# Cross attention and mixture of experts on one core: scores in three PSUM banks, steps of up to 1536 columns, two score buffers for three

## The reference

```
q = ln(x) @ Wq;  k, v = split(concat(ctx, ln(x)) @ Wkv)      # 1178 keys, 1024 queries
dots = einsum('bhid,bhjd->bhij', q, k) * 16**-0.5
dots = where(j > i + 154, -inf, dots)                        # key j is seen from query j-154 on
x = x + softmax(dots) @ v @ Wout + bout
probs = softmax(ln(x) @ Wg);  each expert takes its 256 best tokens, each token goes to one expert
x = x + weight * (gelu(ln(x) @ W1[e]) @ W2[e])
```

## Time and profile before

| | us |
|---|---|
| median of 3 runs (lowest, highest) | 389.99 (389.31, 390.83) |
| profiled execution: its time | 389.28 |
| profiled execution: span from first to last instruction | 387.4 |
| PE busy | 351.4 (91%) |
| ACT busy | 266.4 (69%) |
| DVE busy | 209.8 (54%) |
| POOL busy | 114.8 (30%) |
| ACTIVATE of `exps` (L845), 192 instructions | 169.0 |
| matmuls of `scores` (L1086) / of `values` (L1107) | 101.4 / 96.9 |

### The profile page before, as it was taken

One profiled execution on the slowest core, in us unless ns is written; L12 is line 12 of the kernel. 1 busy time (PEld: TensorE's weight loads), 2 busy tenths in 40 slices (PEclk: granted clock), 3 DMA queues, 4 the chain that ended last, 5 costly groups with the idle time before them and its releaser, 6 DMA issues.

```text
span 387.4 us, 10936 instructions
## 1 busy us (share of the span) xinstructions
PE 351.4 (91%) x4322; PEld 226.9 (59%) x4322; DVE 209.8 (54%) x724; ACT 266.4 (69%) x386; POOL 114.8 (30%) x157
## 2 busy tenths in 40 slices
PE   8879899999999998999999999892776899999993
PEld 7646455544544444453544444581665899999993
DVE  5949658753555556363645456497777523232330
ACT  2555455699999998999999999525742364545530
POOL 5245655400003020200303022400440745555522
PEclk9999999999999999999999999998685999999998
DMA  7534984340347626544448524504530322223100
GB/s 248 156 111 124 284 224 164 124 167 4 98 121 244 150 57 168 156 121 118 114 128 246 128 49 122 195 2 152 174 111 2 100 87 92 82 93 96 58 25 30
DMA packets 37325, 47.68 MB, mean 123 GB/s; under 512 B 8764, under 2 KB 26610, under 8 KB 37265
## 3 DMA queue, kind: packets, MB, share of 16 engines
q1 hardware_dynamic: 34368, 40.26, 35.3%
q0 software_dynamic: 2560, 6.30, 5.2%
q10 hardware_dynamic: 337, 0.32, 0.3%
HBM read 32.71 MB, written 13.81 MB: 120 GB/s over the span
## 4 chain that ended last, share of the span: by engine, by line
PE 67%; DVE 12%; ACT 11%; issue 3%; SPq 3%; DMA 1%; POOL 1%; POOLq 0%; DVEq 0%; ACTq 0%
PE ps L1107 15%; PE ps L1086 14%; PE ps L1287 9%; ACT pbuf L845 9%; PE ps L1299 8%; PE ps L1071 8%; PE ps L1024 5%; DVE v_st L1724 2%; SPq L546 2%; DVE pbuf L1597 2%; PE ps L992 2%; DVE stats L1631 1%; DVE xe L1626 1%; PE ps L1276 1%; DMA k_st<-k_cut 1%
## 5 line engine op out<-in xcount | busy, mean ns | idle before, releaser
L845 ACT ACTIVATE pbuf<-ps 128x1024 f32<-128x1024 f32 (+3 forms) x192 | 169.0, 1030 | 3.1 <-PE ps L1086 3.1
L1597 DVE SCALAR_TENSOR_TENSOR pbuf<-pbuf,seen 128x128 f32<-128x128 f32 (+2 forms) x288 | 75.5, 303 | 63.5 <-ACT pbuf L845 63.0
L1086 PE MATMUL ps<-q_st,k_st 98*32 98x512 bf16 (+4 forms) x2048 | 101.4, 318 | 3.0 <-ACT pbuf L845 2.5
L1107 PE MATMUL ps<-pbuf,v_st 128*32 128x512 f32 (+4 forms) x1024 | 96.9, 473 | 2.9 <-DVE pbuf L1597 2.8
L1086 PEld LDWEIGHTS ps<-q_st,k_st 98*32 98x32 bf16 x2048 | 52.0, 96 | 68.5 <-ACT pbuf L845 25.7
L713 POOL TENSOR_TENSOR mid<-mid 64x1024 f32<-64x1024 f32 x7 | 16.6, 2372 | 122.8 <-DMA mid<-reciprocals 102.5
L1107 PEld LDWEIGHTS ps<-pbuf,v_st 128*32 128x32 f32 x1024 | 27.4, 109 | 28.2 <-issue 11.4
L1287 PEld LDWEIGHTS ps<-mid,piece_f 128*128 128x128 f32 x320 | 38.7, 192 | 1.6 <-issue 0.7
L1287 PE MATMUL ps<-mid,piece_f 128*128 128x128 f32 x320 | 39.0, 275 | 0.5 <-issue 0.5
L1299 PE MATMUL ps<-pbuf,mid 128*128 128x256 f32 x160 | 37.7, 379 | 0.0
L1071 PE MATMUL ps<-mid,pbuf 128*128 128x512 f32 (+1 forms) x80 | 32.5, 542 | 4.7 <-ACT mid L806 4.1
(11 more groups left out here) (250 smaller groups left out, 375.0 us busy)
## 6 DMA issues: line engine op xcount, KB each, us to landing
wts<-in_L_ffn_W SPq DMA_DIRECT2D x16, 512.0 KB, 5.2
k_st<-k_cut SPq DMA_DIRECT2D x48, 147.2 KB, 3.0
q_st<-q_cut SPq DMA_DIRECT2D x48, 128.0 KB, 2.9
q_cut<-wts SPq DMA_DIRECT2D x8, 384.0 KB, 3.6
k_cut<-wts SPq DMA_DIRECT2D x8, 384.0 KB, 3.1
token_rows<-xe SPq DMA_DIRECT2D x4, 512.0 KB, 4.1
mid<-mid SPq DMA_DIRECT2D x28, 64.0 KB, 2.4
mid<-reciprocals SPq DMA_DIRECT2D x28, 64.0 KB, 2.3
```

The source lines that it names most:

```text
L845: nc.scalar.activation(pbuf[:, s % 2, r, c0:c1], st_ps[(s * GH + r) % NST][:, c0:c1], ACT.Exp, scale=SCALE).then_inc(exp_done, 1)
L1086: last = nc.tensor.matmul(st_ps[(s * GH + r) % NST][c:c + 32, a:z], k_st[pa][:, r, t * P + c:t * P + c + 32], q_st[pa][:, r, q0 + a - c0:q ...
L1107: last = nc.tensor.matmul(o_ps[32 * r:32 * r + 32, a:z], v_st[pa][:, t, r, :], pbuf[:, s % 2, r, a + dc:z + dc], start=(t == 0), stop=(t = ...
L1597: last = nc.vector.scalar_tensor_tensor(a, a, 3.0e38, seen[:, off:off + w], ALU.min, ALU.mult)
```

## The change

The steps become four of up to 1536 columns (three banks), so that each head has four scores blocks and four ACTIVATEs a group. Two score buffers of three banks take the place of three of two. The values of a step are cut into three parts, each behind one head's scores: first the upper 512 queries of the step's first tile, which need no mask, so this part waits on the exponentials alone; then the other upper pieces, then the lower ones. `take_outputs` moves behind the masks of heads 0 to 2 of step 0, and the reciprocals to step 3 (in the last group step 2, before head 2). `pbuf` becomes eight separate slots: five in `flat`, two in `w2_sb`, one in `mid`. So the first exponential waits for `lx_done`, and the early second weights are loaded after the last values.

```diff
-NST = 3
+NST = 2
-STEP_TILES = [[0], [5, 6], [4, 7], [3, 8, 9], [1], [2]]
+BW = 3 * 512
+STEP_TILES = [[0, 6], [1, 7, 8, 9], [3, 4], [2, 5]]
...
+def parts(step):
+    pieces = [(t, a, z, c0 - q0) for (t, q0, c0) in step for (a, z) in split_at_bank(q0, S)]
+    first = [p for p in pieces if p[0] == step[0][0] and p[1] == 512]
+    upper = [p for p in pieces if p not in first and p[1] >= 512]
+    return first, upper, [p for p in pieces if p[1] < 512]
...
+        pb_at = ([flat[:, i * BW:(i + 1) * BW] for i in range(5)] + [w2_sb[:, i * BW:(i + 1) * BW] for i in range(2)]
+                 + [mid[:, NB * KT * S + 2 * S:NB * KT * S + 2 * S + BW]])
...
-        st_ps = [ps[:, 1024 * i:1024 * i + 1024] for i in range(NST)]
-        o_ps = ps[:, 1024 * NST:1024 * NST + 1024]
+        st_ps = [ps[:, BW * i:BW * i + BW] for i in range(NST)]
+        o_ps = ps[:, BW * NST:BW * NST + 1024]
...
-                elif g == 4:
-                    second_weights(range(0, E_EARLY))
             sp.wait_ge(v_in, 2 * NG)
             second_weights(range(E_EARLY, E))
+            sp.wait_ge(pv_done, 2 * NG * NSTEP + 2)
+            second_weights(range(0, E_EARLY))
...
+            act.wait_ge(lx_done, NB)
             for g in range(2 * NG):
                 exps(g)
...
-            def values(pa, s, g0, half):
-                pieces = VALUE_PIECES[s][half]
-                if s == 0:
-                    ...
-                    pe.wait_ge(exp_done, (g0 * NSTEP + s) * GH + GH + NST)
-                else:
-                    pe.wait_ge(mask_done, g0 * ((NSTEP - 1) * GH) + s * GH)
+            def values(pa, s, g0, part):
+                if part > 0:
+                    pe.wait_ge(mask_done, (g0 * NSTEP + s + 1) * GH)
+                else:
+                    if s == 0:
+                        ...
+                            pe.wait_ge(raw_done, g0)
+                        pe.wait_ge(v_in, g0 + 1)
                     pe.wait_ge(exp_done, (g0 * NSTEP + s) * GH + GH + NST)
...
                 for s in range(NSTEP):
-                    for r in range(NST):
+                    scores(pa, s, 0, g0)
+                    for r in range(1, GH):
                         scores(pa, s, r, g0)
-                    values_before(0, pa, s, g0, before_g)
-                    scores(pa, s, NST, g0)
-                    values_before(1, pa, s, g0, before_g)
+                        values_before(r - 1, pa, s, g0, before_g)
...
-            def masks(g0):
-                for s in range(1, NSTEP):
+            def masks(g0, before_g):
+                for s in range(NSTEP):
...
-                    if g0 > 0 and s == NSTEP - (3 if g0 == LAST else 2):
+                    if 0 < g0 < LAST and s == NSTEP - 1:
                         reciprocals(g0 - 1)
                     for r in range(GH):
+                        if s == 0 and r == GH - 1 and before_g is not None:
+                            take_outputs(before_g)
+                        if g0 == LAST and s == NSTEP - 2 and r == 2:
+                            reciprocals(g0 - 1)
```

More of the change, by code:

```diff
@@ L64 @@
 for _tiles in STEP_TILES:
-    _col = first_query(_tiles[0]) if len(_tiles) == 1 else 0
+    _col = 0
     STEPS.append([])
@@ L69 @@
         _col += S - first_query(_t)
-    assert _col <= S
+    assert _col <= BW
 NSTEP = len(STEPS)
@@ L93, in split_at_bank, with masked @@
     return out
[L96 to L104, removed]
+def parts(step):
[3 more added lines that the diff above has]
+    return first, upper, [p for p in pieces if p[1] < 512]
+VALUE_PIECES = [parts(step) for step in STEPS]
+NPART = 3
+def masked(t, q0):
+    return (0, 0) if t == 0 else (2 * P - M, M - P) if t == 1 else (min(P, S - q0), 0)
+assert all(a >= q0 + masked(t, q0)[0] for step, ps in zip(STEPS, VALUE_PIECES)
+           for (t, q0, c0) in step for (u, a, z, d) in ps[0] if u == t)
 LAST = NB * NG - 1
@@ L1090, in scores @@
                 last.then_inc(st_ready, 1)
-            def values(pa, s, g0, half):
-                pieces = VALUE_PIECES[s][half]
-                if s == 0:
[L1097 to L1101, removed]
+            def values(pa, s, g0, part):
[3 more added lines that the diff above has]
+                    if s == 0:
+                        for jn in range(len(JOBS) - 2, len(JOBS)):
+                            free_bank(jn)
+                        if g0:
+                            pe.wait_ge(raw_done, g0)
+                        pe.wait_ge(v_in, g0 + 1)
                     pe.wait_ge(exp_done, (g0 * NSTEP + s) * GH + GH + NST)
-                else:
-                    pe.wait_ge(mask_done, g0 * ((NSTEP - 1) * GH) + s * GH)
-                for (t, a, z, dc) in pieces:
+                for (t, a, z, dc) in VALUE_PIECES[s][part]:
                     for r in range(GH):
                         last = nc.tensor.matmul(o_ps[32 * r:32 * r + 32, a:z], v_st[pa][:, t, r, :],
-                                                pbuf[:, s % 2, r, a + dc:z + dc],
+                                                pbuf(s, r)[:, a + dc:z + dc],
                                                 start=(t == 0), stop=(t == STEP_TILES[-1][-1]), skip_group_check=True)
-                if half == 1:
+                if part == NPART - 1:
                     last.then_inc(pv_done, 1)
-                elif g0 == LAST and s == NSTEP - 1:
+                elif part == NPART - 2 and g0 == LAST and s == NSTEP - 1:
                     last.then_inc(pv_upper, 1)
@@ L1140, in maxima, with values_before @@
                 pe.wait_ge(sh_in[pa], g0 // 2 * (16 * GH) + 16 * GH)
-            def values_before(half, pa, s, g0, before_g):
+            def values_before(part, pa, s, g0, before_g):
                 if s > 0:
-                    values(pa, s - 1, g0, half)
+                    values(pa, s - 1, g0, part)
                 elif before_g is not None:
-                    values(1 - pa, NSTEP - 1, before_g, half)
+                    values(1 - pa, NSTEP - 1, before_g, part)
             def group(pa, g0, fl, before_g=None):
@@ L1171, in wout @@
                 last.then_inc(wo_ready, 1)
-            pe.wait_ge(exp_done, 2 * NG * NSTEP * GH + NST - 2)
+            pe.wait_ge(exp_done, 2 * NG * NSTEP * GH + NST - 1)
             pe.wait_ge(scaled, NG)
             pe.wait_ge(extra_done, 2)
-            for half in range(2):
-                values(1, NSTEP - 1, 2 * NG - 1, half)
+            for part in range(NPART):
+                values(1, NSTEP - 1, 2 * NG - 1, part)
             wout(0)
@@ L1611, in group @@
                     take_maxima(pa, g0)
-                if before_g is not None:
-                    take_outputs(before_g)
-                masks(g0)
+                masks(g0, before_g)
             seq(nc.vector.memset(mx, -3.0e38))
```

15 lines of the change are left out of this document (8 added, 7 removed).

## The result

| | before | after |
|---|---|---|
| median of the runs (lowest, highest), us | 389.65 (389.28, 390.83) | 403.98 (402.67, 405.67) |
| ratio to before, 95% interval | | 1.0385 (1.0351 to 1.0419) |
| profiled execution: time / span | 389.28 / 387.4 | 403.08 / 401.3 |
| first exponential / end of the last | 74.06 / 245.32 | 74.37 / 258.31 |
| periods of groups 0 to 7 (first exponential to first exponential) | 20.99, 21.08, 21.67, 22.32, 21.07, 21.07, 21.10, 21.96 | 20.87, 22.61, 22.82, 24.33, 23.27, 23.39, 24.18, 22.47 |

Slower by 14.3 us, where 10 were forecast (the times in the before column are of runs beside those of after, on the same chip). The last period ends with the last exponential.

The account below looks back on a forecast made before the run. ACT was taken to bound the steady group, with SP's staging chain a second bound 0.7 us away. Terms +0.2, -0.2, +5.9, +3.5, 0 and +0.7 gave +10.1 on 389.28; forecast 400.0 us, range 393 to 404.

Parts of the forecast that it names:

- case A: Attention groups: staging comes late and masks are held behind scale; 400 us, own range 397 to 403.5, chance 0.5.
- staging late, groups 1 to 6: SP's chain starts 1.63 us later behind the last values, so the next group's k_st lands late: +5.9 us.
- held masks: Step 0: POOL's scale holds the mask of head 2, delaying the copy and SP's chain: +3.5 us, bounds 0 and 7.
- clock: Rival: PE's waits at group ends lower the clock, adding some 1 us to six groups; 406 us, chance 0.08.
- end: Behind the last exponential: more columns of last values, and scale may hold the last masks; +0.7 us.
- The walk to the copy: Step 0 walked from the first exponential: the copy in take_outputs begins at 4.56 us rather than 2.93.
- By the offsets it hits in groups 2, 5 and 6 ... and perhaps 7: Step 0: scale holds the mask of head 2 in these groups, costing 1.4, 0.8 and 1.3 us.
- PE now waits 2 to 4 us at a group's end: Group ends: PE stands idle this long, which might lower the clock granted at 1.00 through all of the attention.
- Two buffers: Scores wait for the exponential two before: 20.8 us a group where ACT alone would need 20.5.
- case C: Rival: late staging is hidden anyway, groups take 21.0 us; 387.6 us in all, chance 0.08.
- The moved weights: Three early second weights loaded behind the last values: 0 us; without cover one landing, some 3 us.
- case B: Rival: staging late but masks not held, since a mask that begins first isn't held; 396 us, chance 0.27.

Follow-up runs that it names:

- e7: The kernel after, with the loads of the three early second weights made twice: 403.59 us, ratio 1.035.
- the last kernel: e10 with POOL's scale of group g also waiting for the masks of step 0 of group g+2: 384.13 us, ratio 0.9872.
- e10: The kernel after with early staging, the copy in two halves, values in four parts and a ninth probability slot: 389.35 us, ratio 0.9985.

## Why the prediction was off in size, step by step

Direction, place and mechanism were those of case A, but the loss was larger: 403.98 lies at the very end of the range, 4 us above the forecast, and the growth of 14.3 us over the runs beside it is more than the 14.0 that the range leaves above 389.99. Against the terms of the sum:

| term | forecast | measured |
|---|---|---|
| start | +0.2 | +0.3 |
| group 0 | -0.2 | -0.1 |
| staging late, groups 1 to 6 | +5.9 | +5.3 (the kernel with `scale` moved) |
| held masks | +3.5 | +5.2 in groups 1 to 6 (an estimate: 6.95 less 1.8) |
| clock | 0 (its own rival) | +1.8 in group 3 (an estimate) |
| group 7 | 0 | +0.5 |
| end | +0.7 | +0.9 |

**The walk to the copy** was right: 4.56 forecast, 4.72 in group 1 of after, and where no mask was held ahead of it 4.57 in the kernels with late staging and 4.71 in those with early staging. **Staging** came out a little lower than forecast: in the kernel with `scale` moved SP's chain from `sums_away` to its last k_st took 12.0 us on average (11.01 to 12.45), for 12.2 before.

**The step that failed is "By the offsets it hits in groups 2, 5 and 6 ... and perhaps 7".** A hit cost what was forecast: the copy slipped by 1.0 to 1.6 us (0.8 to 1.9 forecast). But in after it hit in all six groups that have a `scale`, five of them in groups 2 to 6, where the sum had three; the copies' slips there sum to 6.8 us, of which the periods show 5.2 for the 3.5 of the forecast. I had moved each group's old distance between the last k_st issue and `scale` into the new period, which left groups 3 and 4 out. That distance did not stay: in group 3 it was 9.7 us before and 7.8 in after, since the last `den` DMA took 3.9 us to land before and 2.1 in after; in group 4 it was 8.7 and 9.0, but the low clock of group 3 had pushed the first exponential back too, to 5.9 us behind that issue, for 4.0 to 4.8 in the others. The landings vary from one execution to the next, and the rows of one execution cannot say which group is hit: after hit six of six, the same attention in e7 five of six.

**The clock** was given 0.08 as a rival that ends at 406, with all six groups slowed and at a group's end. It fell in one group, behind the wait for the copy, and cost about as much (1.8 us) as the masks missed by. In e7 it fell in one group too, group 2, which took 24.26 us. At the group's end PE waited less than the 1 to 4 us forecast: over 0.4 us only in four groups, 0.7 to 1.6. In groups 2 to 6 PE had already lost 0.95 to 1.6 us to the copy in step 0 or 1, so less was left for the end. The step "PE now waits 2 to 4 us at a group's end" was wrong.

**Two buffers**: forecast 20.8 us a group, and 21.0 with the wait for the copy if staging were hidden (case C, 387.6 us in all). With the chain freed and the copy first it is 21.18, with the copy halved 21.08, and 390 us: even without any lateness the change equals before. The ACT time it frees is real: the last kernel takes 20.3 to 20.7 us a group, 20.5 on average, as the forecast had for ACT alone (its 0.83 ns a column and 0.065 us an instruction give 20.4). But it takes finer parts of values to reach it.

**The moved weights** at 0, and the new wait on `lx_done` at 0, were right. Every held mask of after started behind `scale`, by 0.17 us (group 3: 144.41 and 144.58) to 0.76 (group 4), so the escape of case B, a mask that begins first, never came up in it. With the Trainium skill's rule ("SBUF — State Buffer", Who interferes with whom: whoever issues first goes through) the holds agree. Other runs show its other half: each mask that began ahead of `scale` and was still running when it started took 0.26 to 0.29 us, its usual time. Group 6 of the kernel with early staging is such a case (DVE, then POOL; the next mask, from 205.57, was held).

```profile
204.32 0.29 DVE L1616 SCALAR_TENSOR_TENSOR pbuf<-pbuf,seen 128x128 f32<-128x128 f32 x1 [0.84 <-ACT pbuf L861]
```

```profile
204.49 2.37 POOL L729 TENSOR_TENSOR mid<-mid 64x1024 f32<-64x1024 f32 x1 [17.28 <-DMA mid<-reciprocals]
```

## What to carry to other kernels

When a change makes one chain set the period, what hangs on the same chain comes at nearly the same place of every period: what was an occasional collision can become one in almost every group. Nearly is not always: the place still moves by the spread of the DMA landings (0.6 us in one execution here, 1.2 in another). Price such a collision for all groups and for none as the two bounds, and do not decide group by group from the rows of one execution. Each wait that it causes also brings a chance of a low clock, which is a term of its own.

A saving on one of two nearly full engines comes only if the order of the other's work lets it through: with two buffers, the longest run of other work between two blocks that fill them is the number to look at. And moving one producer (staging) moved the multiply behind it onto other masks: after each mend, look again at where POOL's long instruction falls.

## What the runs showed of the hardware

- A hold on DVE does not need POOL's multiply: in the kernel with `scale` moved, `load_v` on POOL (a copy of 128x640, 0.84 us at 147.71) held another mask: one of the five from 146.33 took 0.80 us, from 147.90 on. The copy from PSUM to SBUF took 1.21 to 1.24 us with or without `scale` beside it.
- The granted clock fell to 0.50 for some 3.4 us after PE had waited 1.60 us in after's group 3, and to 0.61 on average over 4.4 us after a wait of 2.28 us in the kernel with the copy first. It fell likewise after 1.86 us in the kernel before with early staging, and after 1.53 us in group 2 of e7. Other waits left it at 1.00: 1.59 us in after, 1.53 and 1.57 in e7, 1.64 and 1.63 in the two kernels with the late chain, and 1.74 in e10 (243.80). Between 1.53 and 1.74 us the length of the wait does not tell; what does is open. The row is from e7, behind its first wait of 1.53 us.

```profile
127.00:128.00 1.00, 1.00 (x24) 0.80 (x20) 0.00 (x0) 0.00 (x0) 0.00 (x0) 0.50 0.62 159
```
